# A fused attention and expert kernel: the expert weights are loaded after all attention operands, and one routing step of the last group moves behind the first two sends

## The reference, cut to what matters

```python
x = x + tanh(g_xattn) * attention(layernorm(x), ctx, ctx, mask)     # 16 heads of width 8, 32 batches x 128 rows
logits = layernorm(x) @ gate_w                                      # 8 experts
expert_weights, expert_indices = top_k(softmax(logits), 2)          # two experts of each row, renormalised
for i in range(8):
    h = silu(xn @ w1[i]) * (xn @ w3[i])                             # 128 -> 512
    out = out + (h @ w2[i]) * wi[..., None]                         # wi: weight of expert i, 0 where not chosen
x = x + tanh(g_ffn) * out
```

## Time and profile before

| what | value |
|---|---|
| median of 3 runs | 460.7 us (459.81 to 461.96) |
| the profiled execution | 459.81 us, of which the span of its instructions is 458.1 us |
| mean granted TensorE clock | 0.972 |
| busy in the span | PE 407.4 us (89%), DVE 290.9 (64%), POOL 259.4 (57%), ACT 239.6 (52%) |
| DMA | 46.24 MB, mean 101 GB/s |

### The profile page before, as it was taken

One profiled execution on the slowest core, in us unless ns is written; L12 is line 12 of the kernel. 1 busy time (PEld: TensorE's weight loads), 2 busy tenths in 40 slices (PEclk: granted clock), 3 DMA queues, 4 the chain that ended last, 5 costly groups with the idle time before them and its releaser, 6 DMA issues.

```text
span 458.1 us, 14422 instructions
## 1 busy us (share of the span) xinstructions
PE 407.4 (89%) x4547; PEld 360.1 (79%) x4548; DVE 290.9 (64%) x786; ACT 239.6 (52%) x564; POOL 259.4 (57%) x312
## 2 busy tenths in 40 slices
PE   2879979999999998997879899988999999999970
PEld 1647658877777776776669799888999999999960
DVE  3876798887888887889546368544444554554420
ACT  2758506667677675766666534233444444444430
POOL 5743554334654737473646568776666665655560
PEclk9989979999999999999999999999999999999995
DMA  7964557457766666485223233334444343333235
GB/s 215 279 123 94 96 96 185 90 105 113 170 147 136 152 134 161 106 216 169 65 69 75 45 52 48 54 67 61 69 70 58 44 54 46 46 47 40 24 29 189
DMA packets 74783, 46.24 MB, mean 101 GB/s; under 512 B 8608, under 2 KB 71490, under 8 KB 74562
## 3 DMA queue, kind: packets, MB, share of 16 engines
q1 hardware_dynamic: 59072, 34.84, 33.2%
q0 software_dynamic: 12272, 8.92, 14.9%
q10 hardware_dynamic: 3392, 1.88, 1.7%
HBM read 18.12 MB, written 14.20 MB: 71 GB/s over the span
## 4 chain that ended last, share of the span: by engine, by line
PE 62%; DMA 9%; issue 7%; DVE 6%; ACT 6%; POOL 4%; ACTq 2%; POOLq 1%; DVEq 0%
PE ps_scores L1612 20%; PE ps_max_scores L1620 10%; DMA sums_scratch<-yt,xg 8%; PE ps_values L897 7%; PE ps_max_scores L853 6%; PE ps_scores L883 5%; PE ps_scores L837 3%; PE ps_max_scores L837 2%; POOL expert_rows_scratch L1328 2%; PE ps_out L921 1%; ACT xn L474 1%; DVE rsplit L1119 1%; ACT w_all L464 1%; DVE qkf L558 1%; POOL sums_scratch L1733 1%
## 5 line engine op out<-in xcount | busy, mean ns | idle before, releaser
L1733 POOL DMA_INDIRECT sums_scratch<-yt,xg x71 | 115.9, 1633 | 66.9 <-DMA sums_scratch<-yt,xg 28.1
L1612 PE MATMUL ps_scores<-xgT,qs 128*128 128x128 f32 x1136 | 141.1, 278 | 5.1 <-ACT xgT L1658 3.8
L1612 PEld LDWEIGHTS ps_scores<-xgT,qs 128*128 128x128 f32 x1136 | 134.1, 194 | 7.1 <-ACT xgT L1658 4.5
L1699 DVE TENSOR_TENSOR qs<-qs,ps_scores 128x512 f32<-128x512 f32 x71 | 48.8, 688 | 88.4 <-PE ps_scores L1612 70.5
L1119 DVE TENSOR_REDUCE rsplit<-ps_max_scores 128x4 f32<-128x512 f32 x128 | 84.8, 685 | 15.0 <-PE ps_max_scores L837 11.2
L1328 POOL DMA_INDIRECT expert_rows_scratch<-xr,pos x64 | 66.4, 1037 | 25.6 <-issue 13.1
L1620 PE MATMUL ps_max_scores<-w_all,qs 128*128 x568 | 75.6, 276 | 2.8 <-ACT yt L1669 2.3
L1620 PEld LDWEIGHTS ps_max_scores<-w_all,qs 128*128 128x128 f32 x568 | 69.0, 192 | 3.8 <-issue 3.6
L1027 ACT ACTIVATE pT<-ps_scores 128x1024 f32<-128x1024 f32 x64 | 62.0, 1022 | 18.1 <-PE ps_scores L837 17.8
L1662 ACT ACTIVATE qs<-ps_scores 128x512 f32<-128x512 f32 x71 | 42.3, 596 | 30.3 <-PE ps_scores L1612 30.3
L1669 ACT ACTIVATE yt<-ps_max_scores,xg 128x128 f32<-128x128 f32 x71 | 26.1, 368 | 60.4 <-PE ps_max_scores L1620 40.4
(11 more groups left out here) (202 smaller groups left out, 527.8 us busy)
## 6 DMA issues: line engine op xcount, KB each, us to landing
qs<-w_all SPq DMA_DIRECT2D x96, 64.0 KB
ks<-w_all SPq DMA_DIRECT2D x96, 64.0 KB
w_all<-in_L_ffn_w_dram SPq DMA_DIRECT2D x24, 256.0 KB
xg<-expert_rows_scratch SPq DMA_DIRECT2D x71, 65.0 KB, 1.9
xs<-in_x_dram SPq DMA_DIRECT2D x4, 512.0 KB, 5.6
sums_scratch<-xs SPq DMA_DIRECT2D x8, 256.0 KB, 4.5
sums_scratch<-yt,xg POOLq DMA_INDIRECT x71, 3.3
expert_rows_scratch<-fill SPq DMA_DIRECT2D x16, 65.0 KB, 2.5
```

The costliest lines, as they stand in the source:

```text
L1612: ins = nc.tensor.matmul(bank[u % 2][:, c * P:(c + 1) * P], w13[:, u % 2, n, c * P:(c + 1) * P], xgT[:], start=True, stop=True)
L1699: nc.vector.tensor_tensor(hidT[:, u % 2], act_s[:, u % 2], ps_b[u % 2], ALU.mult).then_inc(hid_ready, 1)
L1733: pool.indirect_dma_start(out=z_d, out_offset=bass.IndirectOffsetOnAxis(ap=xg_u[:, u, X_IDX:X_IDX + 1], axis=0), in_=yt[:, u % YRING], in_ ...
```

## The change

SP issues no weights between the halves. All eight experts are loaded after the last half, expert g followed by the `begin_sums` of group g (up to g = 5). The eight `store_fill` move the other way, one behind each half of groups 4 to 7. The cap of four weight transfers in flight stays. On POOL `route_std(LAST)` and `route_tokens(LAST)` move from `after`, ahead of the first send, into `late(1)`, behind `send(1)` and the scatter of t = 1.

```diff
-            def load_weights(e, n):
-                if n == 0:
-                    for p in range(2):
-                        sp.wait_ge(qk_loaded[e % 2][p], (e // 2 + 1) * (16 * LOADS))
-                count = 3 * e + n
-                if count >= WEIGHTS:
-                    sp.wait_ge(w_loaded[count % WEIGHTS], 16 * (count // WEIGHTS))
...
+            def load_expert(e):
+                for n, (to, src) in enumerate((
+                        (w_sb_all[:, e, 0:F], w1[e]), (w_sb_all[:, e, F:2 * F], w3[e]),
+                        (w_sb_all[:, e, 2 * F:].rearrange("p (c d) -> p c d", d=D),
+                         w2[e].rearrange("(c f) d -> f c d", f=P)))):
+                    count = 3 * e + n
+                    if count >= WEIGHTS:
+                        sp.wait_ge(w_loaded[count % WEIGHTS], 16 * (count // WEIGHTS))
+                    sp.dma_start(to, src).then_inc(w_loaded[count % WEIGHTS], 16)
...
-            for e in range(2):
-                for n in range(3):
-                    load_weights(e, n)
             for g in range(2, NG):
                 sp.wait_ge(parts_ready, g + 1)
                 for p in range(2):
                     sp.wait_ge(scored, ((g - 2) * GB + (p + 1) * (GB // 2)) * NB)
                     load_half(sp, g, p)
-                    if g >= 3:
-                        for n in (range(0, 1), range(1, 3))[p]:
-                            load_weights(g - 1, n)
-            for n in range(3):
-                load_weights(NG - 1, n)
-            for g in range(BEGUN):
-                begin_sums(sp, range(g, g + 1), 0)
-            for e in range(E):
-                store_fill(e)
+                    if g >= 4:
+                        store_fill((g - 4) * 2 + p)
+
+            for g in range(NG):
+                for p in range(2):
+                    sp.wait_ge(qk_loaded[g % 2][p], (g // 2 + 1) * (16 * LOADS))
+                load_expert(g)
+                if g < BEGUN:
+                    begin_sums(sp, range(g, g + 1), 0)
...
                 if t < GB:
                     scatter(Group(AFTER, 2), (GB + t,))
+                if t == 1:
+                    route_std(LAST)
+                    route_tokens(LAST)
...
                 place_rows(Group(AFTER, 2))
                 scatter(Group(AFTER, 2), range(GB))
-                route_std(LAST)
-                route_tokens(LAST)
```

## The result

| kernel | median | ratio to before |
|---|---|---|
| before | 460.04 us (455.82 to 462.57, 22 runs) | |
| changed | 462.77 us (460.80 to 466.01, 22 runs) | 1.006 [1.004, 1.008] |

The changed kernel is slower by 2.7 us. Its profiled execution has a span of 459.7 us, 1.6 more than that of before. That execution took 461.38 us, 1.4 under its kernel's median, so it shows less of the loss than the medians do. A second profile of the same kernel, taken with the last experiments (`f0`), has a span of 460.8.

What follows compares the result with a forecast made beforehand. POOL's chain of sends was taken to bound the kernel until about 312 us, then PE alone. Weights 0, attention 0 and routing step +2.7 on 459.81 gave 462.5, as a median 463.4 (461.8 to 465.2); overall range 458.5 to 469.

Steps and rivals of the forecast that it cites:

- ACT's stall: ACT, first normalised rows of the last group: waits 7.6 us for POOL's moved `route_std`, until 253.5.
- PE: PE in the expert tiles: tiles 6.9 us late, restart at half clock +1.9, less 1.0 and 1.9 at later pauses.
- Lead: Tile 10 left ACT 4.07 us before its send; stalled, `send(10)` starts 0.8 behind the tile, +2.7, and that stays.
- the two terms of the sum: Moving the weights to the end of SP's queue costs 0; moving POOL's routing step behind `send(1)` costs +2.7 us.
- attention costs nothing: Weights out from between the halves: 0 us, POOL's scatter waits being covered; refuted if attention ends over 1 us earlier or later.
- Rival (a): Attention: scatters land sooner, POOL's 20.3 us of waits shrink by half, -10.1, giving 453.3 us; chance 0.15.
- The slack of the weights: End of attention: all weights landed by 226, 3.6 us before DVE needs them at 229.64, so cost 0.
- second slack: SP's queue: the twelve `xg` loads end at 237, before the last sums can go at 240.24; also 3.6 us.
- Rival (c): Start of the experts: weights land at 235.6 and DVE waits, +5.9 plus ACT's stall, giving 469.3 us; chance 0.15.
- The first send: POOL: freed of the routing step, `send(0)` waits only for the last sums and starts at 243.7, 1.3 us earlier.
- The chain's own +1.1: POOL's sends: with the routing step behind `send(1)`, `send(2)` starts at 255.6 instead of 254.52.
- Rival (b): PE's lead swallows ACT's stall, leaving only the send chain's 1.1: 461.8 us or less; chance 0.26.

Runs made afterwards that it cites:

- f0: The changed kernel itself, run again beside weights-only and stall-only kernels on one chip: 463.88 us, 1.0071 of the kernel before.
- f2: Changed kernel with the routing step back ahead of the first send, and ACT made to wait for the second send's landing: 462.94 us, 1.0045 of before.
- e2: Kernel before with only the routing step moved behind the second send and its scatter, weights still between the halves: 1.0091 of before.
- e1: Changed kernel with the routing step back ahead of the first send, so only weights and padding stores moved: 0.9982 of before.
- f1: Weights-only kernel again, routing step at its old place, on one chip with the changed and stall-only kernels: 459.50 us, 0.9982 of before.
- e3: Changed kernel with ACT's normalised rows moved from tiles 3 and 4 to 6 and 8, their copy from 5 to 9: 1.0037 of before.
- e4: Changed kernel with `route_std` back ahead of the first send, only `route_tokens` behind the second: 0.9978 of before.
- e5: Changed kernel with two weight transfers in flight instead of four, on another, slower chip: 1.0122 of before.

## Why the prediction was right

The time, 463.4, is 0.6 us over the measured 462.77, and slower was the likeliest sign. All of the 0.6 comes from the kernel before, 460.7 in three runs and 460.04 in 22; the difference was forecast at 2.7 and measured at 2.7. That it agrees so well is partly luck, as the terms show. Two slips of the working change no conclusion: 278.3 and 0.8 are 279.1, which is 2.6 behind 276.48 and not 2.7, and of the length of the range 461.8 to 465.2 a third, not a fifth, lies under 463.0. Step by step:

**ACT's stall: right.** Forecast: 7.6 us, ending at 253.5. Measured: 7.35, ending at 252.0, the attention having ended 1.4 us earlier. POOL is named in front of it, and `f2` shows that this wait alone, with PE's restart behind it, costs 3.4 us.

**PE: right.** Forecast: tiles 6.9 late and a restart at half clock, +1.9. The next `up` behind the restart comes 27.01 us after the first (258.62 less 231.61); before it was 18.20 (251.17 less 232.97). That is +8.8, the sum of the two terms. The pause in front of `odds` gave back 1.0 as forecast (36.88 less 29.06 is 7.8), and no second fall of the clock 1.4 instead of 1.9: tile 10 is 6.4 us late, forecast 5.9.

**Lead: right in kind, and it gives way earlier.** 6.4 less the lead of 4.07 and plus 1.14 between tile and send (forecast 0.8) is 3.5 for send 10, forecast 2.7; the second profile gives 4.1. From there it stays as forecast: send 18 is 3.2 us late in the one, 4.1 in the other. What I did not see is that send 7 meets its late tile first: it is already 2.6 us late (37.99 us after the first `up`, 35.41 before), and send 10 adds 0.9.

**Mis-sized, and made up for: the two terms of the sum.** The routing step costs more than 2.7: `e2` says 0.91% of 460, 4.2 us, with an interval from 2.7 to 5.7. The weights' move was put at 0, and gives something that no single measurement tells from 0: 0.18% in both of its comparisons, 0.8 us. In the two profiles of the changed kernel attention ends 1.4 us earlier. That is over the 1 us that I had named as a refutation of "attention costs nothing", so this part of the mechanism (weights out from between the halves cost and give 0) has failed by its own test. The profiles close on this account: attention less 1.4 and send 18 plus 3.2 make 1.8, and the span grew by 1.6; in the second profile less 1.4 and plus 4.1 make 2.7, and it grew by 2.7.

**Why attention ends earlier is open.** Rival (a) said: scatters land sooner. They did (20.3 us of waits became 7.9), and its price of 10 us did not come: over the last seven batches, beside the full stream, attention takes 36.74 us in the changed kernel and 36.73 before (first exponential at 190.06 and 191.43, last at 226.80 and 228.16). The 1.3 us come at one batch, from 173.5 to 179.3 where it was 173.6 to 180.7. That batch isn't the cause in general: `e2`, with the weights between the halves as well, goes from 175.6 to 180.6 there and is late before it. Among the kernels of the first chips with the weights last, six profiles of eight have their first `up` between 231.1 and 231.7; but `e1` has 234.10 and `f1` 232.96, and both kernels with the weights between the halves have 233.0. So the move may be what gives it, and isn't needed to lose it.

**The slack of the weights: sized too large.** I gave them 3.6 us. The chain of `f1` goes through five flights of weights, of 4.2 to 7.1 us each, where I had taken 3.3 for one in the full queue. Its last weight is issued at 226.2, and DVE waits 2.12 us instead of its usual 0.93. The chain then runs through SP's loads of rows, which end at 240.62, to the last sums at 240.66 and the first send: the sums are 7.70 us behind the first `up`, where they were 7.27 before. So the second slack, that of the loads, is used up there too, as in `e3` (7.81). Two pieces of that chain, DVE's row, and SP's:

```profile
214.97 4.20 DMA w_all<-in_L_ffn_w_dram
219.18 7.05 DMA w_all<-in_L_ffn_w_dram
```
```profile
231.75 1.44 DVE L1553 COPY qs<-w_all 128x1024 f32 x2 [2.12 <-issue]
```
```profile
227.75 12.87 SPq L1564 DMA_DIRECT2D xg<-expert_rows_scratch  x12
240.66 1.69 SPq L790 DMA_DIRECT2D sums_scratch<-xs  x2
```

In front of DVE's copy `e3` and `e4` show 1.82 and 1.77. So in three profiles of eight the weights came some 0.8 to 1.2 us late. Rival (c) had the right place, at a fifth of its price of 5.9.

**The first send: right for the reason given.** It waited for the last sums (4.35 us, the sums named), and the step in front of it was cover. Counted from the first `up` it gained 0.7, not 1.3: the sums had landed 3.2 us after their first issue, as forecast (238.87 to 242.10), but the send started 0.87 behind the landing, where I had put 0.2. In `e2` it gained nothing (12.12 for 12.03), the issue of the last sums having taken 1.95 us. The chain's own +1.1 at the third send came out as +1.0 (22.52 less 21.55), and is hidden behind the stall: `f2` is late without it.

**Rival (b), the lead swallows the stall,** fell: the lead took 4.07 of tile 10's 6.4, and the rest went to the end.

## What to carry to other kernels

A step that looks like a delay in front of one consumer may be the input of another: before it is moved behind a wait, list who waits for its counts, and price the engine that waits latest with all that is queued behind it. A stall on an engine off the critical path costs what it exceeds the lead of the next stage by; here the lead was 4.07 us, and the restart of an idle TensorE came on top with 1.9. And look for the second delay behind the first: with ACT's wait away (`e3`), a wait for a late send stood in its place, and no gain could be told.

## What the runs showed of the hardware

A restart of PE shows in the time of its next `up`: 3.56 to 3.79 us where the clock was at 0.50 (1.2 GHz; windows of the kernel before, the changed one, `f2` and `e3`), 2.05 where it was at 1.00 (`e1`, `f1`). It was slow behind every wait for turned rows of 5.78 us or more in this stage (seven of seven profiles that have one), and behind none of 1.25 to 1.31 us (nine of nine). Between them the length of the last wait does not decide: behind 2.23 us the `up` took 3.66 us in the kernel before and 3.63 in `e4`, but 2.05 in `e1` with the same 2.23, and in `f1` with 2.19. Two more were slow behind a short last wait, and in both PE had stood longer shortly before: in `e3` (3.78 behind 1.81) for 2.34 us in front of `down`, and in `e5`, whose weights came late, the first `up` took 3.30 behind 0.87 and waits of 2.63 and 1.83. So 1.6 us of the difference between two profiles of this stage can hang on one restart. Two rows have the same wait, the one of the kernel before in the earlier trace rows, and this one of `e1`:

```profile
263.32 2.05 PE L1604 MATMUL ps_scores<-xgT,qs 128*128 128x128 f32 x16 [2.23 <-ACT xgT L1650]
```

The same pair of sum stores took SP from 0.93 us to 2.09 us to issue in different profiles (0.93 in the changed kernel, 1.69 in `f1`, 2.09 in `e3`), and the stores landed later with it (a median of 2.6 us from issue to landing, 3.4 and 3.2). Where the first send waits for them it starts 11.36 us after the first `up` in the changed kernel, 12.64 in `f1` and 13.07 in `e3`. There is one profile of most kernels, so it is open whether this goes with the kernel or with the execution.
